# The spread copy of the softmax reciprocals: on ScalarE between two exponentials, where it was on GpSimd behind the reorders

## What is computed

```
Q = (x @ Wq.T).reshape(b, h, t, d)        # b=2, h=16, t=1024, d=16; K and V alike
scores  = einsum('bhqd,bhkd->bhqk', Q, K)  # causal mask, then / sqrt(d)
weights = softmax(scores)
ctx     = einsum('bhqk,bhkd->bhqd', weights, V)
return ctx.transpose(0, 2, 1, 3).reshape(b, t, e) @ Wp.T + bp
```

## Time and profile before

| | |
|---|---|
| median of 3 runs | 1603.19 us |
| profiled execution: its own time, its span | 1605.04 us, 1603.5 us |
| mean granted TensorE clock over the span | 0.874 |
| busy over the span: PE, DVE, ACT, POOL | 79%, 56%, 46%, 32% |
| first attention | about 208 to 577 us of the span |
| busy there: PE, DVE, ACT, POOL | 304.52, 228.74, 175.47, 115.12 us of 369.00 |
| granted clock there | 0.76 |

### The profile page before, as it was taken

The page is one execution under the profiler, slowest core; times in us unless marked ns, Lnnn a source line. Parts: engine busy times, 40 slices in busy tenths (PEclk is TensorE's granted clock), DMA queues, the critical chain, the costliest instruction groups (busy, mean ns, idle before and its releaser), DMA issues. The chain is left out here.

```text
span 1603.5 us, 22609 instructions
## 1 busy us (share of the span) xinstructions
PE 1262.6 (79%) x7428; PEld 893.8 (56%) x7428; DVE 895.1 (56%) x2331; ACT 734.5 (46%) x1668; POOL 520.2 (32%) x556
## 2 busy tenths in 40 slices
PE   2675729888888838677699999997575999999977
PEld 1564714433333317466576666765564677777656
DVE  6656538766666533343666666661243666666640
ACT  1544403555454620452566666650153666666640
POOL 0221233333233110040355555530050555555520
PEclk8797955888777968788899999998797999999998
DMA  2213187554453049301111111005102111111005
GB/s 78 109 60 123 56 99 64 55 59 58 51 59 37 22 153 269 112 2 63 47 37 37 37 37 37 27 14 158 49 1 85 25 39 38 39 39 39 18 28 157
DMA packets 133157, 101.02 MB, mean 63 GB/s; under 512 B 48240, under 2 KB 120368, under 8 KB 132784
## 3 DMA queue, kind: packets, MB, share of 16 engines
q1 hardware_dynamic: 132000, 98.53, 27.4%
q10 hardware_dynamic: 1040, 1.05, 0.2%
HBM read 56.30 MB, written 34.87 MB: 57 GB/s over the span
## 5 line engine op out<-in xcount | busy, mean ns | idle before, releaser
L748 POOL TENSOR_SCALAR a_p<-a_p,a_rl 128x128 f32<-128x128 f32 (+7 forms) x256 | 215.6, 842 | 400.1 <-DVE a_rl L690 400.1
L731 ACT ACTIVATE a_p<-psum,a_nm 128x128 f32<-128x128 f32 (+7 forms) x256 | 189.5, 740 | 107.5 <-DVE a_nm L684 106.9
L1225 ACT ACTIVATE a_pt<-psum 128x512 f32<-128x512 f32 (+3 forms) x384 | 166.9, 492 | 154.3 <-PE psum L1098 152.8
L1088 PE MATMUL psum<-a_op_k,a_op_q 64*128 64x512 f32 (+3 forms) x384 | 162.6, 510 | 52.9 <-POOL a_op_k L1023 32.1
L781 PE MATMUL psum<-ident,a_p 128*128 128x128 f32 x1152 | 170.1, 275 | 31.8 <-DVE a_pt L717 31.8
L803 PE MATMUL psum<-a_pt,v 128*64 128x256 f32 (+1 forms) x1280 | 158.9, 370 | 1.1 <-ACT a_ot L817 1.1
L781 PEld LDWEIGHTS psum<-ident,a_p 128*128 128x128 f32 x1152 | 129.6, 140 | 53.5 <-issue 48.3
L684 DVE CUSTOM_DVE_ANT_0 psum<-psum,mask_a 128x128 f32<-128x128 f32 (+3 forms) x128 | 63.8, 499 | 149.4 <-PE psum L766 149.3
L1098 PE MATMUL psum<-a_op_q,a_op_k 64*128 64x512 f32 (+3 forms) x384 | 134.7, 455 | 0.0
L715 ACT ACTIVATE a_pt<-psum 128x256 f32<-128x256 f32 (+2 forms) x192 | 87.4, 455 | 94.8 <-PE psum L781 93.8
L1088 PEld LDWEIGHTS psum<-a_op_k,a_op_q 64*128 64x128 f32 x384 | 79.6, 235 | 90.3 <-issue 32.3
(11 more groups left out here) (257 smaller groups left out, 2810.7 us busy)
## 6 DMA issues: line engine op xcount, KB each, us to landing
a_swap<-a_raw SPq DMA_DIRECT2D x64, 128.0 KB, 2.3
ot_d<-a_ot SPq DMA_DIRECT2D x16, 512.0 KB, 2.6
o_ot<-ot_d SPq DMA_DIRECT2D x16, 512.0 KB, 6.2
a_raw_q<-qk_d SPq DMA_DIRECT2D x48, 128.0 KB, 5.1
a_raw_k<-qk_d SPq DMA_DIRECT2D x48, 128.0 KB, 9.5
a_wf<-wf_d SPq DMA_DIRECT2D x16, 384.0 KB, 3.2
qk_d<-p_stage_h SPq DMA_DIRECT2D x8, 512.0 KB, 2.7
qk_d<-p_stage_l SPq DMA_DIRECT2D x8, 512.0 KB, 3.4
```

What stands on the lines that cost most here:

```text
L731: e.activation(s.p[:, t % NPB, 0:(i + 1) * P], C.score[t % 2][:, 0:(i + 1) * P], ACT.Exp, scale=-1.0, bias=s.nm[:, k:k + 1], accum_out=s.l ...
L748: e.tensor_scalar(s.p[:, t % NPB, 0:(i + 1) * P], s.p[:, t % NPB, 0:(i + 1) * P], s.rl[:, k:k + 1], 1.0, ALU.mult, ALU.mult).then_inc(s.no ...
L1088: e.matmul(bank_a("score", g, k)[:, 0:k1 - k0], q[rows(hd), hd % 2, i * P:(i + 1) * P], kk[rows(hd), hd % 2, k0:k1], start=True, stop=True ...
L1225: e.activation(pt[:, k // G0 % NPT, hd, off:HALF], bank_b("score", g, k)[:, off:HALF], ACT.Exp, scale=-1.0).then_inc(exped, 1)
```

## The change

The spread copy leaves POOL's program, where its three calls are removed, and stands in ACT's as an activation with the function Copy, ahead of the exponential of slot 30 (chunk 0) and of slot 14 (chunk 1). Its two waits, for the reciprocals and for the transpose of the chunk before, go with it. Three slot tables change: `turn_back` of chunk 1 from slot 15 to 18, `normalise` of chunk 1 from 17 to 19 and of chunk 0 from 36 to 35. `turn_back` of chunk 0 stays at 34.

```diff
-O_BACK = {34: 0, 15: 1}
-NORM = {36: 0, 17: 1}
+SPREAD = {30: 0, 14: 1}
+O_BACK = {34: 0, 18: 1}
+NORM = {35: 0, 19: 1}
 ...
-                def repeat(g, c):
-                    e.wait_ge(inverted, 2 * g + c + 1)
-                    wait(e, turned_back, 2 * g + c)
-                    spread = rl[:, :, :].rearrange("p i h -> p (i h)").unsqueeze(2).to_broadcast([P, 4 * G0, 32])
-                    e.tensor_scalar(rle[:, :, :, :].rearrange("p i h d -> p (i h) d"), spread, 1.0, 1.0, ALU.mult,
-                                    ALU.mult).then_inc(repeated, 1)
 ...
                 for g in range(NG0):
                     for u in DIAGONAL[:3]:
                         mask(g, u)
-                    if g:
-                        repeat(g - 1, 1)
                     mask(g, DIAGONAL[3])
                     if g + 2 < NG0:
                         reorder(g + 2)
-                    repeat(g, 0)
                     for u in DIAGONAL[4:]:
                         mask(g, u)
-                repeat(NG0 - 1, 1)
 ...
+                def repeat(g, c):
+                    e.wait_ge(inverted, 2 * g + c + 1)
+                    wait(e, turned_back, 2 * g + c)
+                    spread = rl[:, :, :].rearrange("p i h -> p (i h)").unsqueeze(2).to_broadcast([P, 4 * G0, 32])
+                    e.activation(rle[:, :, :, :].rearrange("p i h d -> p (i h) d"), spread, ACT.Copy).then_inc(repeated, 1)
+
 ...
                         if M_OUT.get(t) == 1 and b:
                             maxima_out(g, 1)
+                        which = extra(SPREAD, g, t)
+                        if which:
+                            repeat(*which)
                         if O_OUT.get(t) == 0 and b:
                             output(g, 0)
```

## The result

The changed kernel took 1553.20 us in the median of 4 runs (1551.68 to 1562.74), against 1604.49 us for the kernel before on the same chip. The ratio is **0.9692, 95% interval 0.9648 to 0.9736**: some 50 us faster. The forecast was 1568 with a range from 1555 to 1590. The profiled execution has a span of 1552.9 us.

A forecast was written before the change was run, and what follows sets the result against it. PE was taken to be bound by POOL's late spread and the clock falling after it. Waits 14.2 + clock 20.1 + `normalise` 2 - copies 0.8 = 35.5 us off 1605.0 gave 1569.5, forecast as 1568 (median 1.9 lower), range 1555 to 1590.

The forecast's parts named there:

- What bounds the kernel, and PE's stall: Before `turn_back` of chunk 0, groups 0 to 5: PE waits for POOL's spread, queued behind the reorders; 14.20 us.
- The stall's second price, the clock: From `turn_back` to the last mask, groups 0 to 5: TensorE's clock falls, costing 22.59 us beyond the waits.
- the group that has no reorder: Group 6, the sample without the late spread: 10.08 us from `turn_back` to the last mask, at clock 1.00.
- the 10 to 11 us named as the sign: Expected length of the stretches from `turn_back` to the last mask in groups 0 to 5, with clock near 1.00.
- ACT's copies: Sixteen copies on ACT, 0.63 us each: hidden in chunk 0, some 0.1 us late in chunk 1; cost 0.8 us.
- What is late next: After the change: reorder results still 8 us early, no new stall; elsewhere, maxima or minima might be late next.
- the 8 to 12 named as a sign: Expected total of PE's waits for `normalise` in the new profile, 8 to 12 us.
- the sizing of the clock: Six stretches after `turn_back`: one keeps a low clock like group 0, five run like group 6; 20.1 us back.
- the worth given to the moved slots: `normalise` of chunk 0 one slot sooner: 2 us, bounds 0 to 9.0; `turn_back` of chunk 1 moved: no cost.
- Rival B: Stretches after `turn_back`: the waits go, the clock stays low; 1582 or, with no clock back, 1589 us; chance 0.20.
- all six groups like group 0: Rival B's case where all six stretches have group 0's lower clock: 21.6 us gained, 1582 us; chance 0.15.
- The upper end of the gain: Whole kernel: 36.8 us for stall and clock, 9.0 for `normalise` waits, 2 for spread of medians; range end 1555.

The follow-up runs named there:

- e5: Changed kernel, but PE's `turn_back` of chunk 0 also waits for the end of POOL's reorders (groups 0 to 5): 1588.11 us.
- e4: Kernel before, its stall ahead of `turn_back` of chunk 0 kept but filled with thrown-away transposes on PE (22, in group 0 6): 1590.12 us.
- e3: Changed kernel's slots, but the spread stays on POOL, chunk 0's between the two passes of the reorder: 1552.80 us.
- e12: e1 with PE's two waits for `normalise` filled by thrown-away transposes, eight in slot 37 and five in slot 18: 1555.74 us.
- e1: Changed kernel with the spread on ACT, but `turn_back` and `normalise` in their old slots (34 and 15, 36 and 17): 1581.84 us.
- e8: Changed kernel with `turn_back` and `normalise` of both chunks one slot earlier (33 and 17, 34 and 18): 1546.38 us.

## Why the prediction was right, and where it fell short

- **What bounds the kernel, and PE's stall:** right. The waits of 14.20 us before turn_back are all gone (15.4 to 1.0 us with the end's), and e5 puts them and 35 us of the loss back.
- **The stall's second price, the clock:** right as a mechanism; e4 shows it as a cause, in the row of group 1 and by 14 us of the time. The way to its size, comparing with the group that has no reorder, held for that stretch: the six came to 9.49 or so each, even under the sample's 10.08 and under the 10 to 11 us named as the sign.
- **ACT's copies:** right. 0.63 us each, hidden in chunk 0 and just filling the gap in chunk 1. That the engine is no reason is e3's doing.
- **What is late next:** the reorders' results are in time, as said. The minima are later than before, which the prediction named only as a possibility: PE's waits for them grew from 6.2 to 9.9 us, with 1.6 us more before `turn_back` of chunk 1. The waits for `normalise` fell to 6.0 us, below the 8 to 12 named as a sign.
- **The step that failed is the sizing of the clock**, "22.59 - 2.5 = 20.1 us", and with it the worth given to the moved slots. PE's busy time fell by 34.6 us, not by 20.1. Three things were off. I let one stretch of six keep a low clock; none did, and the six gave back 25.5 us. I counted the clock only from turn_back to the last mask, and 9.1 us came from outside: the kernel before had 0.79 ahead of the `turn_back` of group 4 and 0.85 ahead of that of group 6, which I took as undisturbed. And I priced `normalise` by its wait alone, "Between 0 and 9.0 I take 2 us", with `turn_back` of chunk 1 at nothing. Their direct worth is 3.9 us over six groups (e12 against the changed kernel). Their larger worth, some 26 us, is that they keep the clock up (e1 against e12 and the changed kernel).
- **Rival B** (the waits go, the clock stays low) had the right reason, the waits for normalise in a ring of three banks, which is what e1 suffers from. That e1 took 1582 us, the very figure given for all six groups like group 0, is luck: its first five stretches ran at 1.00 (10.1 us each), and it lost its time in groups 5 and 6. What was missed is that the diff itself shortens these waits. The Trainium skill ("TensorE: Matmul & The Clock Gate", section "A second HAM failure mode: psum-queue depth-cycling") states that short idles between groups of matmuls, as the PSUM banks are cycled through, make the clock go up and down. e1 agrees (0.91 over six groups), but the changed kernel, with the same ring and shorter idles, stays at 0.99 to 1.00. That filling the idles ends the falls is e12's finding.
- **The upper end of the gain** held the clock's 22.59 us as a bound, which it isn't, since 9.1 us came back outside the stretches that it was taken from. So the range ended at 1555, and the result was 1553. That it lies so near has some luck in it: of the 9.0 us that the range allowed for PE's waits for `normalise`, only 0.8 came once the minima had taken their part (6.1 - 3.7 - 1.6), and that room made up for most of the clock that was missed.

## What to carry to other kernels

A copy that one engine needs soon must not stand in another's list behind passes that wait for loads; moving it within the list, into the gap of such a wait, was here as good as another engine. Where TensorE's clock moves, a wait is priced twice, by its length and by the slower matmuls after it, and the second can be the larger: take the difference of whole stretches at either clock, over all of the loop. To find out whether idleness costs clock, fill the wait with matmuls that are thrown away: if the kernel gets faster, shorten the wait. And after a small further gain, look in which stage it lies, as e8 shows.

## What was not expected of the hardware

- Waits of 0.7 and 1.3 us in a group of some 34 us, with none beside them longer than 0.4 us in the steady part, let TensorE's clock fall from 2.4 to 1.2 GHz in some groups and not in others, of the same program and the same execution: e1's groups 1 to 4 kept 1.00 and groups 5 and 6 didn't, and its runs spread over 22 us. The changed kernel, whose waits are 0.7 us and less, still had one such fall in its first profile (0.93 ahead of the `turn_back` of group 3). With these waits filled the four runs lie within 4 us (1553.38 to 1557.21).
- Thrown-away matmuls, which are transposes of the identity, made a kernel 26 us faster (e12 against e1), 1.6% of its time.
